# A graph network's edge sums: a 16-bit table of places, loaded in eights by TensorE

## The reference

```python
sums   = segment_sum(edge_attr, src, num_segments=n)
counts = segment_sum(ones(edges), src, num_segments=n)
agg    = sums / maximum(counts, 1)[:, None]
combined = concatenate([x, agg, u[batch]], axis=1)     # batch is all zeros
h = relu(combined @ W1 + b1)
x = layernorm(x + (h @ W2 + b2))
```

## Time and profile before

| | |
|---|---|
| runs | 801.40, 800.42, 801.16 us, median 801.16 |
| profiled execution | span 799.5 us from first to last instruction; its time outside the span is not given |
| TensorE busy | 745.1 us (93%), granted clock 0.994 of full speed |
| VectorE busy | 716.8 us (90%) |
| ScalarE, GpSimd busy | 501.7 us (63%), 417.1 us (52%) |
| matmuls of line 936 | 6192, 196.1 us busy |
| register loads of TensorE, SyncE | 17 and 17 |

### The profile page before, as it was taken

The page is one execution under the profiler, slowest core; times in us unless marked ns, Lnnn a source line. Parts: engine busy times, 40 slices in busy tenths (PEclk is TensorE's granted clock), DMA queues, the critical chain, the costliest instruction groups (busy, mean ns, idle before and its releaser), DMA issues.

```text
span 799.5 us, 31269 instructions
## 1 busy us (share of the span) xinstructions
PE 745.1 (93%) x11398; PEld 711.5 (89%) x11399; DVE 716.8 (90%) x2382; ACT 501.7 (63%) x998; POOL 417.1 (52%) x410
## 2 busy tenths in 40 slices
PE   8889999999999999999999888989898986899995
PEld 4689999999999999999999888989898986899995
DVE  8999999999999999999896388989898988799995
ACT  1366676666667767667667545555555552688886
POOL 3087777777677787877776400000000002788983
PEclk9999999999999999999999999999999999999999
DMA  6366556666665666656674678999999990012122
GB/s 215 131 210 204 201 202 211 213 215 219 202 219 195 212 220 211 225 205 214 203 210 167 239 227 260 281 282 282 285 283 285 281 277 10 27 52 64 53 66 64
DMA packets 75268, 156.38 MB, mean 196 GB/s; under 512 B 11084, under 2 KB 51277, under 8 KB 75097
## 3 DMA queue, kind: packets, MB, share of 16 engines
q1 hardware_dynamic: 58328, 102.33, 42.5%
q0 software_dynamic: 16896, 53.54, 17.9%
HBM read 95.47 MB, written 60.37 MB: 195 GB/s over the span
## 4 chain that ended last, share of the span: by engine, by line
PE 60%; DVE 30%; issue 5%; ACT 2%; POOL 1%; DMA 1%; DVEq 0%; ACTq 0%; SPq 0%; POOLq 0%
PE ps L858 33%; DVE onehot L1236 18%; PE ps L785 11%; PE ps L936 5%; PE ps L990 3%; DVE pre L1275 2%; DVE perm L1146 2%; DVE stats L1301 1%; DVE weights_z L1296 1%; PE ps L776 1%; PE ps L792 1%; POOL h_low L628 1%; PE ps L811 1%; PE ps L843 1%; PE ps L841 1%
## 5 line engine op out<-in xcount | busy, mean ns | idle before, releaser
L600 POOL DMA_INDIRECT sorted_rows<-payload,idx x264 | 304.8, 1155 | 131.8 <-issue 51.9
L858 PE MATMUL ps<-attr_buf,perm 128*128 128x198 bf16 x3168 | 302.6, 252 | 1.1 <-ACT attr_buf L642 0.8
L858 PEld LDWEIGHTS ps<-attr_buf,perm 128*128 128x128 bf16 x3168 | 288.6, 96 | 6.1 <-ACT attr_buf L642 1.2
L649 ACT CAST payload<-ps 128x792 bf16<-128x792 f32 x264 | 217.9, 825 | 76.7 <-PE ps L858 62.2
L1146 DVE TENSOR_SCALAR perm<-place_of,pos 128x512 bf16<-128x512 int16 x792 | 241.1, 362 | 3.4 <-PE ps L858 2.7
L1236 DVE TENSOR_SCALAR onehot<-node_of,sup 128x256 bf16<-128x256 int16 x903 | 192.4, 284 | 41.9 <-PE ps L936 22.3
L936 PE MATMUL ps<-sup,onehot 128*128 128x64 bf16 (+1 forms) x6192 | 196.1, 193 | 24.7 <-DVE onehot L1236 21.0
L936 PEld LDWEIGHTS ps<-sup,onehot 128*128 128x128 bf16 x6192 | 193.5, 98 | 27.3 <-issue 27.3
L619 POOL TENSOR_TENSOR xs<-xs,b_all 125x256 f32<-125x256 f32 x50 | 37.6, 775 | 209.4 <-DMA xs<-in_x 209.4
L713 ACT ACTIVATE apart<-node_of,sup 128x256 bf16<-128x256 int16 x129 | 65.6, 508 | 94.3 <-PE ps L936 90.2
L785 PE MATMUL ps<-xt,w1x 128*128 128x125 f32 x800 | 99.9, 278 | 5.9 <-DVE pos L1067 3.3
(11 more groups left out here) (150 smaller groups left out, 603.7 us busy)
## 6 DMA issues: line engine op xcount, KB each, us to landing
sup<-sorted_rows SPq DMA_DIRECT2D x129, 396.0 KB, 4.0
attr_buf<-in_edge_attr SPq DMA_DIRECT2D x43, 576.0 KB
out<-weights_z SPq DMA_DIRECT2D x25, 224.0 KB
xs<-in_x SPq DMA_DIRECT2D x12, 448.0 KB
x_stage<-in_x SPq DMA_DIRECT2D x47, 112.0 KB
sorted_rows<-payload,idx POOLq DMA_INDIRECT x264
pre<-jump_d SPq DMA_DIRECT2D x1, 1560.0 KB, 10.4
pre<-first_d SPq DMA_DIRECT2D x1, 780.0 KB, 7.2
```

What stands on the lines that cost most here:

```text
L600: pool.indirect_dma_start(out=sorted_rows, out_offset=bass.IndirectOffsetOnAxis(ap=idx[:, n:n + 1], axis=0), in_=payload[s][:, :], in_offs ...
L649: nc.scalar.copy(payload[s][:, :].rearrange("p (r w) -> p r w", w=PART), slots_p[s % PSUM_BUFS]).then_inc(s_pay, 1)
L858: last = nc.tensor.matmul(slot_p[s % PSUM_BUFS][r].rearrange("p (h f) -> p h f", f=PLANE), places, parts(a, t * CB + s), start=(t == 0 and ...
```

## The change

The table becomes 16-bit: `where_d`, `where_row` and `where` are `U16` in place of `I32`, and `where_row` is allocated first, so that it lies at another place in SBUF. SyncE's loads read the same number of registers as before, now 16-bit values. TensorE no longer loads sixteen registers at the head of a turn. It has two sets of eight; `find_tables(0, ...)` fills the first set once before the loop and then ahead of super 12 for the next turn, `find_tables(1, ...)` fills the second set ahead of super 4. The tail has no load of its own.

```diff
@@ constants
+AHEAD = PAIR_BUFS // 2
+assert 2 * SUPER_PAIRS - SUP_TURNS * BODY <= PAIR_BUFS
+assert (ZERO_SUPER + 1) * P < 65536
@@ build
-    where_d = nc.dram_tensor("where_d", [2, SUPER_COLS * P], I32, kind="Internal").ap()
+    where_d = nc.dram_tensor("where_d", [2, SUPER_COLS * P], U16, kind="Internal").ap()
...
+        where_row = sb("where_row", [1, 2 * SUPER_COLS * P], U16)
         ident = sb("ident", [P, P])
...
-        where_row = sb("where_row", [1, 2 * SUPER_COLS * P], I32)
...
-        where = edge_sb("where", [P, 2, SUPER_COLS], I32)
+        where = edge_sb("where", [P, 2, SUPER_COLS], U16)
@@ TensorE
+            def find_tables(half, at):
+                pe.load(table_regs[half * PAIR_BUFS:(half + 1) * PAIR_BUFS], where_row[0:1, bass.ds(at, PAIR_BUFS)])
+
             def super_turn(m, count=BODY):
-                pe.load(table_regs[0:count], where_row[0:1, bass.ds(m * BODY, count)])
                 for k in range(count):
+                    if k == PAIR_BUFS - AHEAD:
+                        find_tables(1, m * BODY + PAIR_BUFS)
+                    if k == BODY - AHEAD:
+                        find_tables(0, m * BODY + BODY)
                     at = pe.snap(table_regs[k], min_val=0, max_val=...)
...
+            find_tables(0, 0)
             with pe.Fori(0, SUP_TURNS) as m:
                 super_turn(m)
             super_turn(SUP_TURNS, 2 * SUPER_PAIRS - SUP_TURNS * BODY)
```

## The result

The changed kernel takes 842.62 us (842.08 to 846.95, 4 runs) against 800.79 us in the same comparison: a ratio of 1.0528, interval 1.050 to 1.0556. It is 42 us slower, far outside the predicted range. The spans of the two profiled executions are 840.1 and 799.5 us.

What follows compares the result with a forecast made beforehand. TensorE's chain was taken as the bound, with 21.7 us of register-load stalls in the summing stage. Afterwards 31 x 0.56 + 2.1 = 19.5 us, a gain of 2.2: 799.0 us by the median, 8-in-10 range 794.5 to 804.5.

Steps and rivals of the forecast that it cites:

- L, from both sides: Length L of TensorE's load of eight 16-bit registers: between 0.507 and 0.79 us, taken as 0.56.
- These agree: Register loads priced by 16-byte pieces: 0.183 us a piece from TensorE's rows, 0.187 from SyncE's.
- The stall of 1.41 us: TensorE's idle at each of 15 turn ends before the change, from count, branch, address and the sixteen-register load: 21.15 us.
- the cover of 0.53 us: Sequencer work hidden because TensorE's sequencer runs 0.50 us ahead of the array, with the next matmul due 0.03 later.
- What is left at the turn's end: Count, branch, address and two register instructions after the change: 0.15 us a turn, 16 times, 2.4 us.
- The sequencer standing still: Assumption that TensorE's sequencer does nothing else while it loads, so half a turn's distance hides nothing.
- 31 L + 2.1: Stalls after the change in us, from 31 new loads and the turn ends, against 21.7 before; break-even at L = 0.63.
- VectorE, DMA and SyncE as no bound: Beside the summing: one-hots need 11.0 us a turn, DMA has over half a turn to spare, SyncE's load lies beside.
- The 0.35 us behind a load: Sequencer time from the end of TensorE's register load to the first weight load, counted the same for each new load.
- Rival 1: Sequencer goes on during a load, both loads hide; DMA transfer of 12.45 us a turn limits the gain: 788.7 us, chance 0.09.
- The rivals on the slower side: Fixed part of a load bought twice a turn: by larger pieces plus registers 803.9 us, chance 0.17; by registers 806, 0.07.
- Rival 3: TensorE's load priced by registers, whatever their width: L = 0.79, 26.6 us of stalls, 806 us, chance 0.07.

Runs made afterwards that it cites:

- experiment three: Kernel before with fifteen more register loads, 32-bit and 16-bit in several counts, behind TensorE's last matmul; only the loads' lengths were read, its time not compared.
- Experiment one: Changed kernel with its table back at 32 bits, loads of eight half a turn ahead kept: 798.32 us against 801.17 of the kernel before, ratio 0.9968.
- six: Kernel before with two 16-bit places per 32-bit word, unpacked by register instructions, one load of eight at the turn's head: 796.05 us, ratio 0.9935.
- seven: Kernel before with two 16-bit places per 32-bit word, unpacked, the turn's one load moved ahead of super 11: 792.83 us, ratio 0.9892.
- ten: Kernel before, 32-bit table, four loads of four registers a turn, placed between two matmuls inside supers: 826.02 us against 843.42, ratio 0.9796.
- experiment four: Kernel before with TensorE's load taken out of the loop, so sums go to wrong places: 781.63 us, ratio 0.9744.
- experiment five: Changed kernel with 32-bit table, its two loads moved from supers 4 and 12 to 7 and 15: 794.75 us, ratio 0.9917 to the kernel before.
- eight: Kernel before, where SyncE alone reads its eight rows through 16-bit elements: 801.38 against 801.13 us, ratio 1.0008.

## Why the prediction was wrong

**The step that failed** is "L, from both sides": L = 0.56, with 0.79 as the upper end. It measured 1.927. Both ends were made of loads of 32-bit values, and of the change from 32 to 16 bits, which no row showed, I had only asked whether fewer bytes save something. I did not ask what else a 16-bit load could be than a 32-bit load of half the bytes. The prediction even had nearly the right number in its hand. The Trainium skill's page "Runtime: NRT & Kernel Launch", section Instruction fetch mechanics, gives some 200 ns per register, and the 16-bit rows show 232 (the page writes of loads from HBM, these are from SBUF). The estimate from it, 1.6 us and 30 us slower, was the nearest of all. I set it aside since sixteen registers took 1.106 us. That row speaks against the rule for 32-bit registers in fours, and for nothing else.

**The fit that looked like proof.** "These agree" was the sentence for 0.183 and 0.187 a piece of 16 bytes. The unit was right for four registers, but the load of two registers, taken as one piece, is two accesses (0.539 in experiment three; one of four is 0.340). TensorE's 0.550 is thus two further accesses of 0.275 and not three of 0.183. SyncE's 0.187 was not taken apart by any run. Two differences from four rows can agree by chance, and these did. Experiment one shows the error at 32 bits: 0.592 and not 0.74.

**What held**, by the same steps. The stall of 1.41 us and the cover of 0.53 us: each of the turns measured in experiments one, six, seven and ten comes within 0.05 us of what they give. What is left at the turn's end, 0.15 us: experiment four came to 781.63 where 781.5 stood. The sequencer standing still, wherever the registers are used: line 938's row, and experiment five. The Trainium skill's page "Perfetto Trace Analysis", section Per-engine timelines, has it so for sequencer-only instructions, and the trace now agrees for a register load (577.3 + 1.938 us, the next instruction at 579.3). The count of 31 loads and the sum 31 L + 2.1: 40.1 us, where the summing stage grew from 219.0 to 258.3 us, by 39.3, and began 1.6 us later. VectorE, DMA and SyncE as no bound: experiments four and eight.

**Small terms off.** The 0.35 us behind a load holds only for even supers (it is 0.13 less at odd ones). Rival 1's limit by DMA, 12.45 us a turn, was wrong: 12.0 was reached. The first load, counted at nothing, does count when it is long: 2.1 us put the stage's first matmul at 454.1, and 452.5 before, of which the load explains 0.8 and the sorting stage the rest.

**The rivals on the slower side** had the sign, but not the reason. Both had a fixed part of about 0.4 us bought twice a turn. It measured 0.07 us for 16-bit registers, and two loads of eight (2 x 1.927 = 3.85 us) cost hardly more than one of sixteen (3.797). Rival 3's form, a price by registers, is right for 16-bit ones, with 0.232 us each in place of 0.039; its "whatever their width" is what experiment one refutes.

## What to carry to other kernels

A register load stopped TensorE's sequencer for its whole length, so preloading early bought nothing by the distance. What hides a load is the lead that the sequencer has over its engine (0.5 us here), and what competes for that cover is everything that the sequencer does up to the next instruction of the engine. Put the load between two instructions that need no wait and no new address, in pieces that fit the cover. Load 32-bit registers in fours, and never 16-bit ones one by one: pack them into words if the table must be small. And where a change alters the kind of an operation, a bound made of rows of the old kind bounds nothing.

## What the runs showed of the hardware

- A register load on TensorE's sequencer: 16-bit values 0.07 us + 0.232 us each; 32-bit values 0.08 us + 0.25 us for each four, and as much for each one left over (loads of 1, 2, 4, 5, 8, 9, 12 and 16; two rows at 0.80 us do not fit). SyncE's: eight 16-bit values 1.82, eight 32-bit 0.53 to 0.70.
- The first load of the summing stage took 0.18 to 0.21 us longer than the later ones of its size in every run looked at (1.296 against 1.106, 2.112 against 1.927, 4.006 against 3.797, 0.511 against 0.333).
- After a stall of 4.1 us in the summing stage TensorE's granted clock was 0.50 for some 3 us of the next turn, each of 15 times; after the stalls of 1.4 us (kernel before, 467 to 655 us) it was 1.00, and after those of 1.8 us too, but for one of them, at 469 us.
- TensorE's sequencer runs 0.50 us ahead of the array with matmuls of 31 ns, and four loads of 0.33 us a turn, between two matmuls, cost 0.05 us each.
- A DMA share of 0.94 at 284 GB/s left room for 314 (experiment four).
